# Layer 1's four products with v of a half issued together, its lanes shifted, and projections on two PSUM banks

## What is computed

```
xn = layernorm(x)                              # 8 batches, 512 rows, 256 columns
q, k, v = split(xn @ Wqkv.T + b)               # 16 heads of 16 dimensions
ctx = causal_softmax(q k^T / 4) v              # attention of the first kind
q2 = conv1d(ctx, conv_w, width 3) + conv_b     # new queries from the first attention's output
ctx2 = causal_softmax(q2 k^T / 4) v            # attention of the second kind, same k and v
out = ctx2 @ out_w.T + out_b
ffn = gelu(x @ U1 @ V1 + b1) @ U2 @ V2 + b2    # done in a stage ahead of the attention
x = x + out + ffn
```

## Time and profile before

| | before |
|---|---|
| median of 3 runs | 2185.07 us |
| the profiled execution, its own time | 2184.84 us |
| its span | 2183.0 us |
| TensorE (PE) busy | 1844.7 us, 85% |
| VectorE (DVE) busy | 1256.3 us, 58% |
| ScalarE (ACT) busy | 1019.4 us, 47% |
| GpSimd (POOL) busy | 363.4 us, 17% |
| mean granted TensorE clock | 0.934 |
| chain that ended last, by engine | PE 60%, DVE 15%, DMA 6%, issue 6%, ACT 5% |

### The profile page before, as it was taken

One profiled execution on the slowest core, in us unless ns is written; L12 is line 12 of the kernel. 1 busy time (PEld: TensorE's weight loads), 2 busy tenths in 40 slices (PEclk: granted clock), 3 DMA queues, 4 the chain that ended last, 5 costly groups with the idle time before them and its releaser, 6 DMA issues.

```text
span 2183.0 us, 31789 instructions
## 1 busy us (share of the span) xinstructions
PE 1844.7 (85%) x10767; PEld 904.5 (41%) x10777; DVE 1256.3 (58%) x3777; ACT 1019.4 (47%) x2048; POOL 363.4 (17%) x555
## 2 busy tenths in 40 slices
PE   3575799999979999994689788989898989989877
PEld 2341355554424444541234343444444444444434
DVE  4554455555554454553552775667575757666653
ACT  0232455655645555563354254445454545444444
POOL 2215211111101121213442100010010101000000
PEclk8557899999999999997799899999999999999999
DMA  7245343334374444413104245255553535452550
GB/s 144 68 141 140 67 83 71 80 72 81 64 203 57 71 62 71 61 28 92 32 20 73 38 57 74 41 75 68 69 74 56 74 53 67 65 78 41 66 59 21
DMA packets 145968, 155.87 MB, mean 71 GB/s; under 512 B 26008, under 2 KB 132784, under 8 KB 145808
## 3 DMA queue, kind: packets, MB, share of 16 engines
q1 hardware_dynamic: 123872, 114.75, 34.0%
q0 software_dynamic: 10048, 14.44, 3.7%
q10 hardware_dynamic: 11888, 24.64, 3.5%
HBM read 55.95 MB, written 33.72 MB: 41 GB/s over the span
## 4 chain that ended last, share of the span: by engine, by line
PE 60%; DVE 15%; DMA 6%; issue 6%; ACT 5%; POOL 4%; SPq 4%; DVEq 0%; ACTq 0%; POOLq 0%
PE p_PV L842 11%; PE p_S L804 8%; PE p_S L825 7%; DVE p_S L1193 5%; PE p_Ma L1017 4%; PE p_Ma L765 4%; SPq L1981 4%; PE p_Mb L896 4%; PE p_S L919 4%; DMA t_R<-ks 3%; PE p_Ma L773 2%; DVE t_rr L1151 2%; ACT t_spl L1603 2%; ACT t_R L1625 2%; POOL idd L1873 1%
## 5 line engine op out<-in xcount | busy, mean ns | idle before, releaser
L1625 ACT ACTIVATE t_R<-p_S 128x512 f32<-128x512 f32 (+1 forms) x1216 | 669.2, 576 | 469.4 <-PE p_S L829 312.1
L1193 DVE CUSTOM_DVE_ANT_0 p_S<-p_S,t_NM 128x128 f32<-128x128 f32 (+3 forms) x1024 | 473.1, 522 | 141.7 <-PE p_S L804 138.8
L804 PE MATMUL p_S<-t_R 96*128 96x512 bf16 (+3 forms) x1536 | 454.8, 338 | 67.0 <-DMA t_R<-ks 34.2
L1199 DVE TENSOR_REDUCE t_mx<-p_S 128x1 f32<-128x512 f32 x512 | 346.2, 686 | 255.2 <-PE p_S L804 242.5
L825 PE MATMUL p_S<-t_R 99*128 99x512 bf16 (+3 forms) x1536 | 466.6, 331 | 16.8 <-ACT t_R L1625 6.5
L842 PE MATMUL p_PV<-t_R 128*17 128x512 f32 (+3 forms) x3072 | 324.1, 494 | 8.9 <-ACT t_R L1625 8.7
L804 PEld LDWEIGHTS p_S<-t_R 96*128 96x128 bf16 x1536 | 135.5, 99 | 393.3 <-issue 167.2
L1839 POOL CAST t_spl<-t_rr 128x512 bf16<-128x512 f32 x80 | 49.0, 612 | 996.7 <-DVE t_rr L1151 996.7
L825 PEld LDWEIGHTS p_S<-t_R 99*128 99x128 bf16 x1536 | 150.2, 98 | 150.8 <-ACT t_R L1625 73.2
L829 PE MATMUL p_S<-t_NM 128*128 128x128 bf16 x1024 | 195.6, 220 | 0.0
L1193 DVE DVE_READ_ACCUMULATOR2_ANT t_mx<- 128x1 f32 x1024 | 144.9, 141 | 0.0
(11 more groups left out here) (236 smaller groups left out, 2114.1 us busy)
## 6 DMA issues: line engine op xcount, KB each, us to landing
t_R<-t_spl SPq DMA_DIRECT2D x480, 128.0 KB
t_R<-in_w ACTq DMA_DIRECT2D x32, 512.0 KB, 8.8
t_R<-ks SPq DMA_DIRECT2D x96, 128.0 KB
ks<-t_spl SPq DMA_DIRECT2D x16, 384.0 KB, 7.4
hTd<-t_NM SPq DMA_DIRECT2D x39, 128.0 KB, 2.2
ysd<-t_NM SPq DMA_DIRECT2D x39, 128.0 KB
t_NM<-hTd SPq DMA_DIRECT2D x39, 128.0 KB, 2.5
ysd<-t_NM POOLq DMA_DIRECT2D x39, 128.0 KB, 3.1
```

Of the source, the lines that this page charges most:

```text
L804: t = self.nc.tensor.matmul(bank[:, z, :], qa[0:96, h, qb * 128:(qb + 1) * 128], ka[0:96, h, 0:n], start=True, stop=True)
L1193: x = nc.vector.tensor_tensor_reduce(out=sc, in0=sc, in1=m.maskq[:, 512 - n:512], scale=1.0, scalar=NEG, op0=ALU.add, op1=ALU.max, accum_o ...
L1199: nc.vector.tensor_reduce(m.mx[:, g, i:i + 1], m.S1[s1_bank(k)][:, :], AX.X, ALU.max).then_inc(s.s1_read, 1)
L1625: nc.scalar.activation(m.P1X[kb][j0 // per] if u.causal else m.P[p % 2][:, j0:j0 + per, :], m.s2_bank(k)[:, 0:per * n].rearrange("p (j n) ...
```

## The change

Four edits, all with effect in layer 1 alone:

1. The products with v of a half are issued in one go: `expp` marks the half as late only at kb = 3, and `finish` issues all four products, behind the second score step of the next half. The probabilities of kb = 0 get a ring of six buffers instead of four (`P1R`, `ring_use`, `p_tile`), since two of the next half's are written before the products of this one; the two more lie in columns of XT that are no longer read.
2. `close` takes one step more, and `maxp` one step more per half, ahead of the transpose of the maxima. A half of `expp` is now 14 turns (13 before), one of `maxp` 13 (12 before).
3. Projections use banks Ma and Mb in turn: k goes to Mb, and so do the second transpose of the context, the second one of the output stage and its second product.
4. `LATE2` is 4 for the first and the last batch alone, and 0 for the six others.

```diff
-LATE2 = 4
+LATE2 = (4, 0, 0, 0, 0, 0, 0, 4)
...
+def ring_use(u, g, j):
+
+    return 8 * (u.n - 16) + 4 * g + j
...
+        self.P1R = self.P1[0] + [self.XT[:, c, 0:512] for c in range(2)]
...
+    def p_tile(self, u, g, kb, j):
+        if not u.causal:
+            return self.P[kb % 2][:, j, :]
+        return self.P1R[ring_use(u, g, j) % 6] if kb == 0 else self.P1[kb][j]
...
     def maxp(self, u):
-        return steps(s1_uses(u))
+        return steps(s1_uses(u) + 2 * u.causal)
...
     def pre1(self, u):
-        return steps(3 if u.kind == 1 else 2 if u.c else LATE2 + 4)
+        return steps(3 if u.kind == 1 else 2 if u.c else LATE2[u.b] + 4)
...
-                self.late = (u, g, kb)
+                if not u.causal or kb == 3:
+                    self.late = (u, g, kb)
...
     def finish(self):
 
-        (u, g, kb), self.late = self.late, None
-        self.product(u, g, kb)
-        if kb == 3:
+        (u, g, last), self.late = self.late, None
+        for kb in range(4) if u.causal else (last,):
+            self.product(u, g, kb)
+        if last == 3:
             yield
             yield from self.close(u, g)
...
     def close(self, u, g):
-        return steps(1)
+        return steps(2 if u.kind else 1)
...
+            yield from steps(u.causal)
             k, self.s1 = self.s1, self.s1 + 1
             e.wait_ge(s.s1_read, k)
             self.nc.tensor.transpose(m.S1[s1_bank(k)][0:16, 0:128], m.mx[:, g, :], m.ident[:, :]).then_inc(s.s1_mm, 1)
...
-            yield from self.project(u, m.XT[:, :, 512 * b:512 * b + 512], (0, 0, 0))
+            yield from self.project(u, m.XT[:, :, 512 * b:512 * b + 512], (0, 1, 0))
             return
         if c == 0:
-            yield from steps(LATE2)
+            yield from steps(LATE2[b])
             for cc in range(2):
-                M = self.mbank(0, s.ct_done, 2 * b + cc + 1)
+                M = self.mbank(cc, s.ct_done, 2 * b + cc + 1)
...
         for h in range(2):
-            M = self.mbank(0, s.out_add, 2 * b + h + 1)
+            M = self.mbank(h, s.out_add, 2 * b + h + 1)
...
+        if u.causal and kb == 0:
+            use = ring_use(u, g, j0)
+            if use >= 6:
+                e.wait_ge(s.pv_mm, 129 + 4 * ((use - 6) // 4))
...
+        elif u.causal and p >= 132:
             e.wait_ge(s.pv_mm, p - 3)
```

More of the change, by code:

```diff
@@ L393, in __init__ @@
                    [R3[:, 1024 + 128 * j:1152 + 128 * j] for j in range(4)]]
-        self.P1X = [[p.rearrange("p (j n) -> p j n", j=1) for p in self.P1[0]],
+        self.P1R = self.P1[0] + [self.XT[:, c, 0:512] for c in range(2)]
+        self.P1X = [[p.rearrange("p (j n) -> p j n", j=1) for p in self.P1R],
                     [p.rearrange("p (j n) -> p j n", j=1) for p in self.P1[1]],
@@ L842, in product @@
             t = self.nc.tensor.matmul(m.PV[32 * j:32 * j + 17, n0:512], vt[:, kb, 4 * g + j, :],
-                                      m.P1[kb][j] if u.causal else m.P[p % 2][:, j, :], start=(kb == 0), stop=(kb == 3),
+                                      m.p_tile(u, g, kb, j), start=(kb == 0), stop=(kb == 3),
                                       skip_group_check=True)
@@ L851, in close @@
             return
+        yield
         i = 2 * (u.n - 16) + g + 1
@@ L1033, in fin1 @@
         for c in range(2):
-            M = self.mbank(0, s.ft_done, 2 * b + c + 1)
+            M = self.mbank(c, s.ft_done, 2 * b + c + 1)
             e.wait_ge(s.ctx_done, 2 * (u.n - 16) + 2)
@@ L1513, in pre1 @@
         if u.kind == 1:
-            yield from self.project(u, (0, 0, 0))
+            yield from self.project(u, (0, 1, 0))
             return
         if c == 0:
-            yield from steps(LATE2 + 2)
+            yield from steps(LATE2[u.b] + 2)
         self.residue(u, 0, m.MB[0], m.CB[:, c:c + 1])
@@ L1617, in scores @@
         e.wait_ge(s.s2_mm, k + 1)
-        if u.causal and p >= 132:
+        if u.causal and kb == 0:
+            use = ring_use(u, g, j0)
+            if use >= 6:
+                e.wait_ge(s.pv_mm, 129 + 4 * ((use - 6) // 4))
+            else:
+                e.wait_ge(s.x2_base, NB)
+                e.wait_ge(s.p_mm, NB)
+                e.wait_ge(s.v_mm, VN[1, 0, 1])
+        elif u.causal and p >= 132:
             e.wait_ge(s.pv_mm, p - 3)
@@ L1625, in scores @@
         nc.scalar.activation(
-            m.P1X[kb][j0 // per] if u.causal else m.P[p % 2][:, j0:j0 + per, :],
+            m.P1X[kb][ring_use(u, g, j0) % 6 if kb == 0 else j0 // per] if u.causal else m.P[p % 2][:, j0:j0 + per, :],
             m.s2_bank(k)[:, 0:per * n].rearrange("p (j n) -> p j n", j=per),
@@ L1726, in pre1 @@
         if u.kind == 1:
-            yield from self.project(u, (0, 0))
+            yield from self.project(u, (0, 1))
             return
         if c == 0:
-            yield from steps(LATE2)
+            yield from steps(LATE2[b])
             for cc in range(2):
@@ L1735, in pre1 @@
                     e.wait_ge(s.qk_mm, QK[NUM[2, b - 1, 1], 0])
-                nc.scalar.copy(m.cT[:, cc, 1:513], m.MB[0][:, :]).then_inc(s.ct_done, 1)
+                nc.scalar.copy(m.cT[:, cc, 1:513], m.MB[cc][:, :]).then_inc(s.ct_done, 1)
                 yield
@@ L1750, in fin1 @@
                 e.wait_ge(s.out_mm, 2 * b)
-            nc.scalar.copy(m.c2T[:, c, :], m.MB[0][:, :]).then_inc(s.ft_done, 1)
+            nc.scalar.copy(m.c2T[:, c, :], m.MB[c][:, :]).then_inc(s.ft_done, 1)
             yield
@@ L2026, in maxp @@
         for g in range(2):
-            yield from steps(len(packs_of(u)))
+            yield from steps(len(packs_of(u)) + u.causal)
             i = 2 * u.n + g
```

2 lines of the change are left out of this document (1 added, 1 removed).

## The result

| | before | after |
|---|---|---|
| median | 2184.75 us (4 runs, 2183.05 to 2189.77) | **2169.82 us** (4 runs, 2167.04 to 2173.84) |
| ratio after / before | | **0.9929**, 95% interval 0.9912 to 0.9945 |
| the profiled execution, its own time | 2184.84 us | 2173.84 us |

The change makes the kernel 0.71% faster. 0.26% had been forecast, which lay inside what counts as no change. The measured gain lies outside that, inside the range of 2154 to 2203 us, and at the lower edge of the 2170 to 2188 us that were given for the case that the walk is right. The profiled execution of after is the slowest of its four.

What follows compares the result with a forecast made beforehand. VectorE was taken to limit halves without projections, TensorE those with them. Terms -27.6 + 17.6 + 2.4 + 0.5 + 2.4 - 1 = -5.7 us against 2184.84 gave 2179 us, 0.26% faster, range 2154 to 2203 us.

Steps and rivals of the forecast that it cites:

- the walk is right: Main case: the new order walked with traced durations gives 2179 us, 2170 to 2188; chance 0.62.
- LATE2 = 0 for six batches: Layer 1, middle batches: six waits for old keys and five slow convolutions behind them go, 27.6 us off.
- The keys are there at about 31.2, the pack stands at 34.4: Timing in us for the earlier first convolution: keys arrive before the next iteration's first pack, leaving 3 us.
- The walk of the pair: First convolution and output stage, now first and second half: 32.85 us against 32.45, +2.4 us for six.
- Products in one go: Block costs TensorE 2.47 us, 0.45 less per half; VectorE idles 1.4 us, bare second halves 9.99 to 10.8, +17.6 us.
- Halves with a projection: Second convolution 17.3 us, +0.5 for six; convolution and output pair +2.4; q, k, v 17.3 against 17.34, 0.
- First halves: First halves of a unit, bare or with two transposes: VectorE idles 2.2 us, three each about 0.8 dearer, +2.4 us.
- VectorE doesn't starve longer: First rival: block costs 2.3 us or packs come sooner, bare halves stay at 10 us, 2159 us; chance 0.16.
- TensorE is the bound throughout: Rival: 0.45 us comes off each of 64 halves instead of 20 us coming on, 2128 us; chance 0.02.
- The keys still late: Rival: SyncE's queue holds the fan late, so the 27.6 us don't come, 2207 us; chance 0.05.
- The block as dear as four apart: Rival: block of products costs 3.0 us, 0.5 us in every half, +32 us, 2211 us; chance 0.06.
- The clock falls in the new waits: Rival: clock falls to 1.2 GHz in 22 waits on Mb or context, 37 us, 2216 us; chance 0.09.

Runs made afterwards that it cites:

- Two goes: Against the kernel before with LATE2 = 0 for the six middle batches: products kb 0 and 1 issued together, 2 and 3 together; 2118.95 us, 0.9704.
- its own experiment: Kernel before with LATE2 = 0 for the six middle batches and projections on two banks, products apart, lanes not moved; 2141.77 us, 0.9810.
- without the moved lanes: The changed kernel with maxp and close back at their old number of steps, the other edits kept; 2161.48 us, 0.9886 of the time before.
- the keys' edit: The kernel before with LATE2 = 0 for the six middle batches and nothing else; alone 2140.35 us, 0.9803.
- the block a step later: Changed kernel with all projections on Ma, its block of four products one pack later and close one turn shorter; 2140.25 us, 0.9806 of before.

## Why the prediction was right, and where it was off

**The bound was read rightly for bare halves, too simply for the others.** Where VectorE is the limit, joining all four products costs (9.98 to 10.68). In halves with q, k, v it gives 0.79 us, but in those with a convolution nothing (17.07 to 17.11, the pair 30.28 to 30.53). In the second convolution's half, as in those with q, k, v, VectorE is then idle for 1.41 us behind the block; the latter have the product moved behind q in exchange. Two goes give something in all of them (16.63, 16.75, 29.79).

**LATE2 = 0 for six batches.** Waits 8 to 2, the second convolution -28.3 us in all against -27.1 forecast (-27.6 and +0.5). "The keys are there at about 31.2, the pack stands at 34.4" held. But the edit was priced alone at 27.6 us and is worth 41. The part that was missed, 13 us of which 9.4 are the transposes' wait for Ma, was inside, in the row at 1538.43, and was used there only as a mark of the clock. The walk of the pair gave 32.85 and the runs 32.85, so the sum did not suffer: the other edits spend there, on the output product's wait for the context and on the longer halves, just what this one wins. The step was right in the sum and wrong as the price of the edit. On top of the three other edits it is worth 25 us (1.0043 to 0.9929).

**Products in one go.** The block cost 2.28 us, not 2.47, so the three joined gaps and drains are worth more than 0.06 us each. VectorE's idle is 1.27 and not 1.4, a bare half 10.69 and not 10.8. **This is the mis-sized term of the sum**: 21 x 0.71 = +14.9 us where "+17.6" stood, for 22 halves; the trace has 21 of them. The first rival had the condition "if the block costs 2.3 us", and that the bare halves then stay at 10 us. The block did cost 2.28 us, and VectorE starved all the same. The Trainium skill's TensorEngine Tiling (Array Packing), under Key Properties, says that a change of tiling mode drains TensorE. The runs agree that fewer changes are cheaper (2.28 us for four joined, 2.41 for two pairs, 2.65 apart); that these 0.1 us a change are drains and not gaps of another kind, they don't show. In bare halves they are worth nothing, and in those with q, k, v they are the smaller part of the gain: two thirds come from the product that moved behind q.

**Halves with a projection.** q, k, v came to 17.16, with 17.3 forecast (-2.2 us for 0). The wait on Mb is 1.40 us where 1.55 had been walked, in 13 halves (14 forecast). The output product's wait is 1.6 us.

**First halves, and what was left out.** "+2.4" stood for three first halves, "each about 0.8 dearer" at 12.0 us. They are 11.90, 11.91 and 13.02 us long, the last with a fall of the clock in it and 11.90 or 11.91 in the three kernels with one go that have none there. But before they were 12.19, 12.19 and 11.78, not 11.2: -0.4. The last half, with the seventh output stage, costs +2.4 and stood in no term; the sum had six. That these two errors nearly cancel is luck.

Left out, too, were the first four distances (-2.4), what lies ahead (-0.8, less than the profiled executions differ by there, 1202.6 to 1208.8 us at the first of these transposes), and the end (-1.2), of which "about 0" had been said. At the end the second bank gives up to 6 us, as its own experiment shows. Two things take from that: with the products in one block behind the last exponential, the last transposes of p_PV come 23.4 us behind the last transpose of the maxima (without the moved lanes) and not 22.1 (apart). And in after's profiled execution the clock fell in that block (4.40 us from its start to those transposes, 3.14 in the kernel with q, k, v on one bank). With the 6.0 us of low clock set aside, the spans differ by -17.0 us, where -5.7 had been forecast. Most of the misses have one sign: bare halves -2.7, q, k, v -2.2, second convolution -1.2, the first four distances -2.4. In the halves that repeat they are 0.1 to 0.2 us each, the size that the forecast had named ("an error of 0.1 us per half would be 6.4 us") and allowed for in either direction.

**The rivals.** "VectorE doesn't starve longer" is refuted by the 1.27 us; the kernel with two goes is what it would have looked like. "TensorE is the bound throughout" falls with the bare halves. "The keys still late" falls with the two waits left. "The block as dear as four apart" falls with 2.28 us. "The clock falls in the new waits" is half true. At the waits of 1.40 and 1.6 us it did not fall, as the six of 1.57 us in before had suggested. It fell elsewhere, behind shorter ones, and in two of the twelve halves with q, k, v: the granted clock below 1.00 there was named as a sign that the prediction is wrong, and so the sign appeared, at 3.9 us in all. See below.

**Where the gain of the keys' edit went.** By intervals: alone 0.9803; with one go and moved lanes 0.9818; with two banks instead 0.9810; with both 0.9929. Neither costs much; together they cost 27.5 us, 24 of them on top of the kernel with one go and moved lanes. Of that, k on the second bank is 12 x 0.61 = 7.3 us. With the products in one go, the output stage's half is 13.33 long with moved lanes alone, 13.27 with two banks alone and 15.04 with both: with both, and only then, its second product waits for the context. That is 1.71 us six times, 10.3; the first convolution's half costs 0.61 six times, 3.7, and the last half 1.7: 23 of the 24 us.

## What to carry to other kernels

Price each edit of a bundle alone, and look for waits at both places when a step moves: where it goes, and where it leaves. What joining instructions on a feeding engine costs is set by what its consumer has in store; join up to that store and no further, and put the larger group behind the last item that the consumer needs. A product that waits for nobody does most where the engine would wait for a bank. A second buffer that serves two kinds of user makes one wait for the other.

## What the runs showed of the hardware

TensorE's clock fell where no forecast had it. Windows of 4 us of after around the half that took 19.91 us instead of 17.16, and TensorE's rows at that fall and at the last one:

```profile
1338.00:1342.00 4.00, 3.31 (x24) 2.06 (x23) 3.06 (x12) 2.43 (x6) 0.00 (x0) 0.73 0.00 0
1342.00:1346.00 4.00, 4.00 (x10) 1.80 (x9) 1.10 (x8) 1.17 (x2) 0.00 (x0) 0.50 0.02 3
```

```profile
1337.09 0.39 PE L818 MATMUL p_S<-t_R 96*128 96x512 bf16 x1 [0.54 <-DVE t_mx L1209]
...
1340.07 0.38 PE L825 MATMUL p_S<-t_ident,t_mx 128*16 128x128 f32 x1 [0.68 <-DVE t_mx L1209]
...
1342.77 3.73 PE L779 MATMUL p_Ma<-t_R,t_WQ 128*128 128x512 f32 x4
...
2107.84 0.38 PE L825 MATMUL p_S<-t_ident,t_mx 128*16 128x128 f32 x1 [0.67 <-DVE t_mx L1209]
```

From 1340.07 on everything runs at 1.2 GHz: the transpose shows 0.38 us instead of 0.28, the projection of q 3.73 instead of 1.94. It is back by 1346.70, and the half is 2.75 us longer. Ahead of the fall lie two short waits, 0.54 and 0.68 us, 3 us apart. The clock falls again at 1370.68, 1981.75 and 2107.84, each time at the transpose at the end of a bare half, behind the same pair of waits. Windows of 4 us from 1320 to the last transpose of the maxima, away from the waits for keys and for the copies of the maxima, show such falls in the profiled executions (one of each kernel) only where the products go in one go: four in after, two with q, k, v on one bank, three without the keys' edit, one with all projections on one bank, all at that transpose and behind those waits; one without the moved lanes, just behind a transpose that waited 1.08; none with the block a step later. Before and the five kernels with products apart or in two goes show none. Most such halves keep 2.4 GHz (after has 21 and four falls), so the pair of waits goes with the falls and isn't the whole cause. The kernel with the block a step later has the wait of 0.67 us in its bare halves and not the one of 0.54, and no fall. What decides stays open.

The Trainium skill's page TensorE: Matmul & The Clock Gate, under A second HAM failure mode: psum-queue depth-cycling, describes such swings from short idle times between groups of matmuls on banks in turn. The traces agree in kind; in size it is 1.1 to 2.75 us a time, 6.0 us in after. Behind the longer waits of 1.4 to 1.6 us, which stand in halves with projections, no fall is seen there.
